# One core, two Mamba-style layers and an MoE: the last chunk's serial stage placed beside the third MoE, with a new order of parts on every engine

## The reference, cut to what matters

```
x1  = LN(x + mamba(x))                    # 2 batches x 1024 tokens x 128, inner width 256, state 16
      mamba: conv(4 taps) -> silu -> dt, B, C -> delta = softplus(.)
             h[t] = exp(delta*A)[t] * h[t-1] + (delta*u*B)[t]      per (channel, state)
             y = sum over 16 states of h*C, + u*D;  y * silu(res);  out projection
x2  = LN(x1 + ffn_fp8(x1))
x3  = LN(x2 + ssm(x2))                    # one delta per token: mean of softplus, 16 states
out = LN(x3 + x3-weighted sum + MoE(RMS-scaled x3))   # 8 experts, top 2, capacity 512, a gated side net
      expert: (gelu(h @ Wg) * (h @ Wu)) @ Wd,  h 128 wide, hidden 256
```

## Time and profile before

| | us |
|---|---|
| median of 3 runs | 533.24 (530.87 to 534.29) |
| the profiled execution | 535.09 |
| its span, first to last instruction | 533.3 |
| busy: PE, DVE, ACT, POOL | 425.3, 419.7, 315.1, 178.6 |

### The profile page before, as it was taken

How to read it: one execution, slowest core, us unless ns; L and a number is a source line. 1 busy time by engine, 2 the same in 40 slices (tenths; PEclk the granted TensorE clock), 3 DMA queues, 4 the chain that set the end, 5 groups by cost and what they waited for, 6 DMA issues and landing times.

```text
span 533.3 us, 5892 instructions
## 1 busy us (share of the span) xinstructions
PE 425.3 (80%) x1680; PEld 256.9 (48%) x1680; DVE 419.7 (79%) x942; ACT 315.1 (59%) x517; POOL 178.6 (33%) x147
## 2 busy tenths in 40 slices
PE   4976667699649999997569999775599995449994
PEld 3322212253235778552245776432367774147883
DVE  3087999997989999698989989978899884334654
ACT  2586552378738976577578785255787832544232
POOL 0056485555163434234163433451534100000000
PEclk9987977799969999999869999969799998656997
DMA  8295768666426354442193554620835000000000
GB/s 300 109 339 175 240 210 263 211 217 202 163 79 200 116 171 161 142 160 78 32 334 133 180 167 132 220 92 20 323 151 175 23 1 1 20 0 1 0 1 20
DMA packets 22064, 74.18 MB, mean 139 GB/s; under 512 B 2320, under 2 KB 4368, under 8 KB 21648
## 3 DMA queue, kind: packets, MB, share of 16 engines
q1 hardware_dynamic: 22032, 73.82, 41.0%
HBM read 72.50 MB, written 1.31 MB: 138 GB/s over the span
## 4 chain that ended last, share of the span: by engine, by line
PE 50%; DVE 21%; issue 13%; ACT 12%; POOL 2%; DVEq 0%; ACTq 0%; POOLq 0%
PE ps_y L475 12%; PE ps_u L608 9%; PE ps_g L564 8%; DVE ps_state L919 6%; PE ps_u L564 5%; DVE product L934 3%; PE ps_state L564 2%; ACT x L703 2%; ACT ps_state L692 2%; DVE stats L944 1%; PE ps_y L608 1%; POOL drive L813 1%; PE ps_g L523 1%; DVE l_state L990 1%; PE ps_g L534 1%
## 5 line engine op out<-in xcount | busy, mean ns | idle before, releaser
L813 POOL TENSOR_TENSOR drive<-du,b_row 128x512 f32<-128x512 f32 x128 | 164.0, 1290 | 208.3 <-DVE ps_state L919 186.0
L475 PE MATMUL ps_y<-product,par 128*128 128x512 f32 x256 | 135.7, 655 | 13.2 <-DVE product L934 12.9
L692 ACT ACTIVATE ps_state<-delta,decay_rate 128x512 f32<-128x512 f32 x128 | 86.2, 687 | 63.9 <-DVE product L934 61.9
L934 DVE TENSOR_TENSOR product<-ps_state,c_row 128x512 f32<-128x512 f32 x128 | 86.1, 680 | 5.5 <-PE ps_y L475 5.3
L919 DVE TENSOR_TENSOR_SCAN ps_state<-ps_state,carry,drive 128x512 f32<-128x512 f32 x64 | 81.5, 1282 | 4.0 <-ACT ps_state L692 4.0
L475 PEld LDWEIGHTS ps_y<-product,par 128*128 128x128 f32 x256 | 48.9, 208 | 70.6 <-issue 37.3
L919 DVE TENSOR_TENSOR_SCAN ps_state<-ps_state,drive 128x512 f32<-128x512 f32 x64 | 77.3, 1219 | 2.3 <-ACT ps_state L692 2.3
L608 PEld LDWEIGHTS ps_u<-wd,hidden 128*128 128x128 f32 x448 | 54.2, 191 | 5.4 <-issue 2.4
L608 PE MATMUL ps_u<-wd,hidden 128*128 128x128 f32 x448 | 54.6, 275 | 0.0
L1092 DVE SCALAR_TENSOR_TENSOR acc<-ps_u,net_weight,acc 128x128 f32<-128x128 f32 x128 | 35.9, 344 | 15.3 <-PE ps_u L608 12.5
L774 ACT ACTIVATE gelu<-ps_g 128x512 f32<-128x512 f32 (+1 forms) x42 | 24.4, 597 | 31.8 <-PE ps_g L564 18.5
(11 more groups left out here) (199 smaller groups left out, 605.4 us busy)
## 6 DMA issues: line engine op xcount, KB each, us to landing
b_row<-bc_dram SPq DMA_DIRECT2D x64, 512.0 KB, 5.0
c_row<-bc_dram SPq DMA_DIRECT2D x64, 512.0 KB, 4.1
x_in<-x_t SPq DMA_DIRECT2D x4, 256.0 KB, 7.0
gelu<-w_gate SPq DMA_DIRECT2D x1, 1024.0 KB, 9.3
hidden<-w_up SPq DMA_DIRECT2D x1, 1024.0 KB, 10.9
wd<-w_down SPq DMA_DIRECT2D x1, 1024.0 KB, 12.8
out<-result SPq DMA_DIRECT2D x4, 256.0 KB, 2.4
par<-params SPq DMA_DIRECT2D x1, 598.0 KB, 6.7
```

Source lines behind the costliest of these rows:

```text
L475: mm(ps_y[:, :], ident, product[:, g % PRODUCTS, :], start=False, stop=(n == STATE - 1)).then_inc(y_pe, 1)
L692: nc.scalar.activation(ps_state[g % RING][:, :], delta[:, c % 2, h, :], ACT.Exp, scale=decay_rate[:, h, n:n + 1]).then_inc(decay_act, 1)
L813: nc.gpsimd.tensor_tensor(drive[:, g % DRIVES, :], du[:, h, :], b_row[:, m % ROWS, n % 2, :], ALU.mult).then_inc(drive_pool, 1)
L934: v.tensor_tensor(product[:, g % PRODUCTS, :], state[:, :], c_row[:, m % ROWS, n % 2, :], ALU.mult).then_inc(product_dve, 1)
```

## The change

It does four things.

1. Tail 3 gets other banks: the scan's three and `ps_y`. Its first matmul waits for the last product and the last scan in place of the MoE of chunk 2. Its intermediate tiles lie in the `product` buffers, not in `gelu`. Hence new waits: the copies into `hn_t` and `hn_parts` (k = 12) wait for the last gate and up matmul of the MoE before; `overflow` waits for the last `accum` before; the second scan's state is single, with a carry copy of one column; `result` now is `acc` itself, so that `acc` of the next chunk waits for the store (`stored`) of the one before.

```diff
+        def tail_bank(c, name):
+            if c == LAST:
+                return {"r1": ps_state[0], "x1t": ps_state[1], "ffn": ps_state[2], "x2t": ps_y, "dlt": ps_state[2],
+                        "bx": ps_state[0], "mean": ps_state[1], "r3": ps_y, "hnt": ps_state[2], "logits": ps_state[1],
+                        "counts": ps_y}[name]
...
                 if k == 0:
-                    if c:
+                    if c == LAST:
+                        pe.wait_ge(product_dve, count(by_vector, STEPS - 1))
+                        pe.wait_ge(state_dve, STEPS)
+                    elif c:
                         pe.wait_ge(hidden_dve, 2 * NETS * c)
                         pe.wait_ge(gelu_act, 2 * NETS * c)
                         pe.wait_ge(acc_dve, NETS * c)
...
                 if k == 12:
                     after(act, tail_pe, c, "hnt")
+                    if c:
+                        act.wait_ge(gate_pe, 2 * NETS * c)
+                        act.wait_ge(up_pe, 2 * NETS * c)
...
                 if k == 15:
                     after(act, tail_dve, c, "xw")
                     if c:
-                        after(act, fin_act, c - 1, "result")
+                        act.wait_ge(stored, 16 * c)
```

```diff
+            def use(name):
+                if table[0] != name:
+                    nc.scalar.preload_act_table_set(name)
+                    table[0] = name
...
-                if e % GROUP == GROUP - 1 and (c < LAST or e == EXPERTS):
-                    nc.scalar.preload_act_table_set(EXP_LN)
```

More of the change, by code:

```diff
@@ L73 @@
[L73 to L76, removed]
[4 rows of a table removed]
[24 rows of a table added]
     },
     "scalar": {
-        "pre": (-15.267, -14.377, -14.369, -14.369, -13.882, -13.064, -12.783, -11.823),
@@ L203, in build, with l1_of @@
         product = sb("product", [P, PRODUCTS, CHUNK])
+        def l1_of(c, name):
+            name = {"ln": "abs", "t": "sp"}.get(name, name)
+            i = L1_NAMES.split().index(name)
+            if c == CHUNKS - 1:
+                place = product[:, i, :]
+            elif i < 6:
+                place = gelu[:, i // 2, i % 2, :]
+            else:
+                place = hidden[:, 1, 0, :]
+            return place[0:STATE, :] if name in ("step", "decay", "drive") else place
         carry = sb("carry", [P, HALVES, STATE])
@@ L335, in block_of, with multiplied, absorbed, count @@
             return ap[:, j * P:(j + 1) * P]
-        def carries(g):
-            c, k = divmod(g, UNITS)
-            return c // PER_BATCH * UNITS + k + 1
+        def multiplied(g):
+            return g % UNITS in MULTIPLIED[g // UNITS]
+        def absorbed(g):
+            return g % UNITS + 1 in PAIRED[g // UNITS]
+        def count(which, g):
+            return sum(map(which, range(g + 1)))
+        def by_pool(g):
+            return multiplied(g)
+        def by_vector(g):
+            return not multiplied(g)
+        def summed(g):
+            return not absorbed(g)
+        def paired(g):
+            return g % UNITS in PAIRED[g // UNITS]
+        def made(eng, g):
+            if multiplied(g):
+                eng.wait_ge(product_pool, count(by_pool, g))
+            else:
+                eng.wait_ge(product_dve, count(by_vector, g))
+        def added(eng, g):
+            if absorbed(g):
+                eng.wait_ge(pair_pool, count(paired, g + 1))
+            else:
+                eng.wait_ge(y_pe, count(summed, g))
+        def carried(eng, g):
+            which = by_pool if multiplied(g) else by_vector
+            eng.wait_ge(carry_pool if multiplied(g) else carry_dve,
+                        sum(which(i) for i in range(g + 1) if i // UNITS % PER_BATCH == 0))
         def blocks_of(ap):
@@ L665, in pre @@
                 else:
-                    for h in range(HALVES):
-                        after(act, pre_act, c, f"abs{h}")
-                        do(pre_act, sp_exp[:, h, :], sp_abs[:, h, :], ACT.Exp, scale=-1.0)
-                    for h in range(HALVES):
-                        after(act, pre_act, c, f"exp{h}")
-                        do(pre_act, sp_ln[:, h, :], sp_exp[:, h, :], ACT.Ln, bias=1.0)
+                    h = k - 7
+                    use(EXP_LN)
+                    after(act, pre_act, c, f"abs{h}")
+                    if h:
+                        after(act, pre_dve, c, "a0")
+                        after(act, pre_act, c, "ln0")
+                    do(pre_act, sp_exp[:, :], sp_abs[:, h, :], ACT.Exp, scale=-1.0)
+                    after(act, pre_act, c, f"exp{h}")
+                    do(pre_act, sp_ln[:, h, :], sp_exp[:, :], ACT.Ln, bias=1.0)
             def split(c, e):
```

354 lines of the change are left out of this document (200 added, 154 removed), and 113 rows, old and new, of the table PLACES.

## The result

| | before | after |
|---|---|---|
| median, us | 533.27 (530.87 to 534.29, 4 runs) | 492.35 (490.83 to 493.75, 4 runs) |
| span of the profiled execution, us | 533.3 | 491.1 |
| mean granted clock of the span | 0.889 | 0.932 |

A forecast was written before the change was run, and what follows sets the result against it. VectorE was taken to bound outside the MoEs, PE inside them, with the serial stretch as the win. Terms summed to -30.9 on the 533.3 us span, -41 of it the serial stretch: forecast 502 us, range 480 to 522.

The forecast's parts named there:

- My 60 us: MoE 2 with tail 3 beside it: 52 to 60 us, upper end taken, so no change; bounds 55 and 70.
- the slower rivals: Tail 3 queues at hand-offs beside MoE 2: 535 to 545 us, 3%; or gain eaten up, 528 to 538, 4%.
- my -41: Serial stretch, tail 3 alone between MoE 2 and MoE 3: it goes, 41 us less.
- The rival that left the last third of tail 3 behind the last net: Tail 3 starts beside MoE 2, its last third stays behind for the k = 12 waits: 510 us, 6%.
- MoE 0 at 57 us: MoE 0: PE loses some 10 finishes, VectorE becomes the bound with 1 us of waiting; 61 to 57 us, -4.
- that -1.5: MoE 1: VectorE stays at 47.5 us, PE falls by some 7 x 0.96; 50 to 48.5 us.
- The price of a unit: Scan on VectorE: 2.05 us a unit in a batch's first chunk, 1.96 in the second; 2.0 used.
- the rival at 10%: All stages fall into step, VectorE keeps some 95% outside the MoE: 482 us and lower, chance 10%.
- my -6.4: From 36 to the first join: -10.4 for splits moved, +1 for their new place, +3 for 1.5 more units.
- The splits: VectorE's splits ahead of delta 0: 10.4 us shed from stretches where it bounds, 1 us charged for the place.
- The table requests: ACT's table loads: 63, before 65, on an engine busy 59%; 0 us.
- The rings and the pre-1 block: Deeper rings against ACT's pre 1 in one run behind three scan steps: set equal, between -5 and +5 us.

The follow-up runs named there:

- e5: Kernel after, with eight finishes of the second scan and nine of the fourth moved forward in PE's queue alone: 518.87 us, ratio 0.973.
- e10: Kernel after, with GpSimd's first du in chunk 0 waiting until VectorE has made both halves of delta: 492.88 us, ratio 0.923.
- e11: Kernel after, with the third table set requested first wherever ScalarE changes its set, 62 more loads: 551.75 us, ratio 1.037.
- e1: Kernel after, with tail 3 put back behind MoE 2 in its old banks and tiles, the rest of the new order kept: 527.38 us, ratio 0.990.
- e8: Kernel after, with the delta steps of chunks 1 to 3 on GpSimd instead of VectorE: 495.13 us, ratio 0.931.
- e13: Kernel after, with carry copies on ACT and delta of chunks 1 to 3 on GpSimd, chunk 2's behind the bias addition: 486.47 us, ratio 0.913.
- e7: Kernel after, with the 64 carry copies of chunks 0 and 2 on ACT instead of VectorE: 487.47 us, ratio 0.920.
- e2: Kernel after, with VectorE's splits back among the units of the first scan, ACT's kept early: 503.62 us, ratio 0.947.

## Why the prediction was right, and by how much not

- **Tail 3 beside MoE 2: right, the size set 4 us too high.** My 60 us ran from the first gate. By that cut MoE 2 took 59.9 us before (382.7 to 442.6) and takes 56.0 now, with tail 3 in it (387.7 to 443.7). The chain of the tail starts 7.9 us behind the first gate (forecast: some 8) and takes 46.1 us from out projection to logits (the lines follow below this point). I had 44.2 at least and 51.9 with the queueing of tail 2; of those 7.7 us of queueing 1.9 came, 0.1 us per hand-off, where the slower rivals needed 1.6. The serial stretch went from 46.2 to 5.4 us, -40.8 against my -41. The sign that I had named for it, a gap under 2 us, was wrong all the same. The rival that left the last third of tail 3 behind the last net had the gap at 8 us because of the waits at k = 12; these are not seen (the copy into hn_t at 438.30 follows the last Gelu of MoE 2 at once, and the logits are there before the last accum). What stays behind is the end of tail 3's routing and the norm of chunk 2, by VectorE's own order.

```profile
395.63 2.05 PE L645 MATMUL ps_state<-par,res_gate 128*128 128x128 f32 x16
441.73 0.18 DVE L1232 TENSOR_TENSOR logits<-ps_state,rms_inv 128x32 f32<-128x32 f32 x1
```

- **MoE 0 and 1: right sign, wrong engine.** I made VectorE the bound of MoE 0 at 57 us. In the trace PE is busy 50.70 of 50.70 and VectorE 47.63, so what PE sheds counts in full: 5.2 us of work, 5.3 of time. For MoE 1 it is 5.0 and 5.3; I had subtracted seven units' passes from PE, where four and a half left, and then let the stretch end by VectorE's 47.5 plus a margin. Two errors lie behind that -1.5, and they do not cancel. e5 shows the limit of such a count: in MoE 0 the passes put back cost what they take, in MoE 1 the new order of almost the same passes cost 18.6 us.
- **The price of a unit: too high.** I added the durations of scan, copy and product to 2.05 us. Start to start a unit takes 1.78 (3.55 for two), since the recorded durations overlap. Thirteen units are 23 us and not 26. That the stretch between MoE 0 and 1 still grew by 26.2 is luck: VectorE's busy time there grew by 30.9 (thirteen products and sixteen scans more, two gatings more, slower steps of delta), and its idle time fell by 4.7. The sign that I had named, 28 to 29 us more of scans there, came (18.7 of scans, 8.8 of products and 1.8 of copies in recorded time), since it was counted in the same durations.
- **The idle time: the rival at 10% came in its condition, not in its time.** It had VectorE at 95% outside the MoEs, and VectorE is at 97% there: its idle time fell from 24.9 to 8.0 us. I took 1 of 8 us off behind MoE 1 and nothing elsewhere. Behind MoE 1 it fell by 6.3 us, which is the whole of the 4.1 that I missed there and more. In the first stretch other things ate it: VectorE's busy time stayed at 123.5 us though 10.4 of splits had gone. Two more scans and a product there account for 1.4, and 6.7 are the slower delta of the next point (9.6 us before the change, 16.3 after it, in this stretch, with the end of delta 0 now behind 36). A third gating is 0.7, and two small operations of the tail that took 1.25 and 1.16 us in place of 0.15 and 0.55 are 1.7. So -6.0 against my -6.4 is luck too.
- **The splits: right in sum, wrong in both parts.** I charged 1 us for the new place. Delta 0 does begin 1.3 us later (29.87 in place of 28.55), but not behind VectorE's splits, which are over at 26.3: VectorE stands 3.56 us for ACT's exponential, and ACT now has all its splits ahead of it. The first scan starts at 37.8 in place of 35.8, with the second half of delta 0 slowed (above). What I could not see in the earlier trace rows is that 0.74 us was not their own duration: with GpSimd at rest it is 0.48. But delta went the other way. Its four steps, over all chunks, took 18.8 us before (3.5 in the earlier trace rows, three of 5.1) and take 27.2 after (5.9, 7.4, 7.4 and 6.5). For 2.9 of these 8.4 us, in delta 0, e10 shows that GpSimd beside them is the cause. For the rest it is likely: at 52.28, for one, a step takes 1.64 us beside a drive that began at 51.57.
- **The table requests: 0 was right for a wrong reason.** The number hardly changed (65 to 63), and that is why it cost nothing. That ACT is "busy 59%" was no cover: an added load costs 0.95 us of its 1.28 in the time (59.4 / 62). The Trainium skill, ScalarE: Activation LUTs, section on what ACT_TABLE_LOAD costs, has 2.66 us for a switch, load and drain. The loads of e11 are 1.28 us each in the trace, as in the earlier trace rows, and less than that arrived, so the measurement decides against the longer price here.
- **The rings and the pre-1 block: set equal.** The waits of the earlier trace rows that the rings were to end are gone, and the one run on rings (in another order, and with one gating moved) makes them worth 9.6 us. The split into two terms stays open.

## What to carry to other kernels

Look for room for a serial tail on the engine that bounds the place where it goes. Here room was made first, by taking scan units out of MoE 2, and this shift by itself gained nothing (e1); that the overlap needs the room is my reading and was not run. Count an engine's free time by what stands behind its waits, not by its share: ACT at 64% and GpSimd at 36% both turned into bounds in some stretches once a wait or a load was put into their queue (e11, e8, e13). Price a sequence of instructions from start to start and not by the sum of their durations (e7). And when two engines' orders are changed, check each product against the order of its consumer: one engine's list moved alone cost 26 us (e5).

## What the hardware showed that I had not expected

A VectorE addition or subtraction of 128x512 with both inputs in SBUF takes 0.69 us with GpSimd at rest and 1.64 beside GpSimd's multiplications, which themselves go from 1.24 to 1.54 us. In this kernel that is seen in delta 0 (0.95 us for each operation, e10) and in the splits (0.48 against means of 0.85 and 0.98 us when they are back among the units, e2). Scans and products, which read one operand from PSUM, kept 1.22 to 1.28 and 0.68 us beside the same GpSimd work. The Trainium skill has the rule on its page SBUF — State Buffer, section on SBUF's two separate sides: whichever of a VectorE operation with two SBUF inputs and a GpSimd operation that reads SBUF starts first holds the shared pair of ports for its whole length, and the other is blocked. By that rule the two would alternate, and the trace agrees in kind: three operations at 32.85, 34.52 and 36.20 us start 1.67 us apart, about 0.4 us more than a drive alone. In size it agrees less well: a drive and an operation one after the other, by their durations alone, would be 1.24 + 0.69 = 1.93 us.

The second thing is that two requests of the same table set in a row leave one load (63 with doubled requests, 63 without), so a request that changes nothing costs nothing; one that changes the set costs 1.28 us on ACT, and here 0.95 us in the end.
